# The last expert's rows added by TensorE with a 0/1 matrix, and two pieces of work moved

## The reference

```python
for i in range(8):                       # layer 0, experts; topk_idx: two experts per row
    mask = (topk_idx == i).any(-1)
    sel = jnp.sort(jnp.where(mask, tok, T))[:capacity]       # 271 rows at most
    yi = gelu(xf[sel] @ w1[i] + b1[i]) @ w2[i] + b2[i]
    out = out.at[sel].set(yi, mode='drop')                   # a later expert replaces an earlier one
x = x + out
h = layernorm(x) @ W                     # layer 1, graph step
a = leaky_relu(h @ attn_l + (h @ attn_r).T, 0.2)
nomi = exp(a - a.max(1)) * adj
x = x + elu((nomi / nomi.sum(1)) @ h)
```

## Time and profile before

| | us |
|---|---|
| median of three runs | 875.61 |
| lowest and highest run | 867.36, 879.09 |
| profiled execution, its own time | 869.55 |
| its span in the trace | 867.7 |

### The profile page before, as it was taken

The page is one execution under the profiler, slowest core; times in us unless marked ns, Lnnn a source line. Parts: engine busy times, 40 slices in busy tenths (PEclk is TensorE's granted clock), DMA queues, the critical chain, the costliest instruction groups (busy, mean ns, idle before and its releaser), DMA issues. The chain is left out here.

```text
span 867.7 us, 13717 instructions
## 1 busy us (share of the span) xinstructions
PE 775.2 (89%) x4212; PEld 585.6 (67%) x4213; DVE 603.2 (70%) x1175; ACT 409.1 (47%) x836; POOL 337.3 (39%) x333
## 2 busy tenths in 40 slices
PE   5999999999999999935999984899958999999994
PEld 4998655555545543424999982687846888888883
DVE  6675867766675679984989865687694656666562
ACT  3345435556555556631666641641332544444451
POOL 2600258668667778434424005000011444333422
PEclk9998979999999999975999995999868999999997
DMA  7538877888887866333345303951472388752110
GB/s 272 202 100 314 208 238 255 272 270 254 279 276 251 282 235 220 128 96 108 137 154 214 124 26 111 433 205 56 169 300 90 67 263 237 240 156 38 31 19 0
DMA packets 61655, 159.02 MB, mean 183 GB/s; under 512 B 20907, under 2 KB 39521, under 8 KB 58403
## 3 DMA queue, kind: packets, MB, share of 16 engines
q1 hardware_dynamic: 40659, 97.97, 33.3%
q0 software_dynamic: 20944, 60.38, 22.6%
HBM read 103.00 MB, written 49.93 MB: 176 GB/s over the span
## 5 line engine op out<-in xcount | busy, mean ns | idle before, releaser
L1868 DVE TENSOR_REDUCE mx<-ps 128x1 f32<-128x452 f32 x264 | 147.8, 622 | 66.3 <-PE ps L1317 65.6
L973 ACT ACTIVATE expo<-ps 128x452 f32<-128x452 f32 x264 | 124.4, 552 | 96.1 <-PE ps L1329 95.2
L1337 PE MATMUL ps<-expo,v_st 128*64 128x452 f32 (+1 forms) x576 | 117.1, 528 | 0.0
L1161 ACT ACTIVATE h<-ps,b_l 128x128 f32<-128x128 f32 x224 | 60.8, 383 | 115.4 <-PE ps L1677 112.5
L1317 PE MATMUL ps<-k_st,q_st 96*128 96x452 f32 x264 | 108.9, 425 | 4.1 <-DVE mx L1868 3.8
L1329 PE MATMUL ps<-q_st,k_st 98*128 98x452 f32 x264 | 96.7, 390 | 3.4 <-ACT expo L973 2.3
L907 POOL DMA_INDIRECT out<-y1t,out_row x29 | 46.1, 1591 | 118.3 <-DVE share L2264 94.7
L1317 PEld LDWEIGHTS ps<-k_st,q_st 96*128 96x128 f32 x264 | 51.1, 194 | 52.6 <-DVE mx L1868 34.7
L1694 PE MATMUL ps<-w_ring,h_hi 128*128 x232 | 82.6, 395 | 1.3 <-DVE h_lo L2276 0.5
L837 POOL TENSOR_TENSOR part_lo<-part,part_hi 128x512 fp32r<-128x512 f32 x64 | 82.3, 1312 | 0.5
L890 POOL DMA_INDIRECT x1t<-x_d,goal x29 | 30.0, 1033 | 128.8 <-DVE goal L2238 110.8
(11 more groups left out here) (352 smaller groups left out, 1793.2 us busy)
## 6 DMA issues: line engine op xcount, KB each, us to landing
w_l<-w_l SPq DMA_DIRECT2D x8, 2053.0 KB, 8.4
part<-w_l POOLq DMA_DIRECT2D x32, 512.0 KB, 6.5
w_split_d<-part_hi POOLq DMA_DIRECT2D x32, 512.0 KB, 5.4
w_split_d<-part_lo POOLq DMA_DIRECT2D x32, 512.0 KB, 3.9
adj<-adj_t SPq DMA_DIRECT2D x22, 704.0 KB, 4.3
w_ring<-w_split_d SPq DMA_DIRECT2D x10, 1365.5 KB, 6.7
w_ring<-w_split_d SPq DMA_DIRECT2D x5, 1365.0 KB, 6.2
w_ring<-w_split_d SPq DMA_DIRECT2D x1, 4096.0 KB, 13.6
```

Source lines behind the costliest of these rows:

```text
L973: act.activation(expo[g % 8][:, :], ps[:, 3 + g % 3, 0:QC], ACT.Exp, scale=SCALE).then_inc(s_exp, 1)
L1161: last = act.activation(h1[:, f, :], ps[:, 4 + f // 4, (f % 4) * P:(f % 4 + 1) * P], ACT.Gelu_apprx_tanh, bias=b1_l1[:, bass.ds(e, 1), f])
L1337: return pe.matmul(ps[at:at + 2 * DK, 6 + g // T % 2, lo:hi], v_st[h % 2][:, kt, :], expo[g % 8][:, lo:hi], start=kt < 2, stop=kt == T - 1 ...
L1868: dve.tensor_reduce(mx4[:, n // KB, n % KB:n % KB + 1], ps[:, i % 3, 0:KC], AX_X, ALU.max).then_inc(s_mx, 1)
```

## The change

Seven experts' results are gathered from memory; the eighth's is not written to memory at all. The gathers wait for the first seven results only, and their bounds check leaves out rows of expert 7, whose tiles keep zeros. ScalarE writes the token numbers plus 128 of all tiles into `numbers` (eleven activations, during the seventh expert). VectorE compares them with `place_of0` of expert 7's three row blocks, which gives `hot_last`, a matrix with a 1 where a slot holds a token. The eighth result is kept in SBUF as a high part `y_hi` (ScalarE) and a low part `y_lo` (VectorE); TensorE multiplies `hot_last` with both, two tiles to a PSUM bank, and VectorE adds each pair of tiles to `x_res` (`last_expert`). VectorE's order after the experts is: comparison, five gathered tiles, low part, two gathered tiles, and then the groups with the other gathered tiles between them. The addition of `u` and the products with the attention vectors stand ahead of the experts. TensorE takes the right and left scores of each group right behind its turning, and the first two features behind the third turning. SyncE's load of the edge weights also waits for the comparison and the high part.

```diff
-RIGHT_BANKS = (7, 7, 3)
+RIGHT_BANKS = (7, 3, 7)
+LAST_AT = (E - 1) * CT
+EARLY_ROWS = 5
...
-        RIGHT_DONE, LEFT_DONE = (1, 3, 4), (2, 5, 6)
+        RIGHT_DONE, LEFT_DONE = (1, 3, 5), (2, 4, 6)
...
+                    if last and k:
+                        continue
                     sp.wait_ge(s_yo, PRIMED + e + 1)
...
             sp.wait_ge(s_y0_ps, PRIMED + E)
+            sp.wait_ge(s_w2lo, E + 1)
+            sp.wait_ge(s_yo, PRIMED + E)
             for t in range(T):
                 sp.wait_ge(s_gath[t], 16)
...
-                pool.wait_ge(s_ys[k], PRIMED + 32 * (E // 2))
+                pool.wait_ge(s_ys[k], PRIMED + 32 * len(range(k, E - 1, 2)))
             for t in range(T):
                 pool.indirect_dma_start(
-                    out=nat[:, t, :], out_offset=None, in_=ys0_d[:, :],
+                    out=nat[:, t, :], out_offset=None, in_=ys0_d[0:SLOTS0 - CAPP, :],
...
+            def token_numbers():
+                act.wait_ge(s_w2lo, E - 1)
+                for t in range(T):
+                    act.activation(numbers[:, t, :], const[:, C_IOTA:C_IOTA + P], ACT.Identity, bias=const[:, C_FAR + t:C_FAR + t + 1])
+
+            def last_rows():
+                act.wait_ge(s_yo_ps, PRIMED + E)
+                act.activation(y_hi[:, 0:2, :], ps[:, 6, :].rearrange("p (s d) -> p s d", d=D), ACT.Identity)
+                act.activation(y_hi[0:CREM, 2, :], ps[0:CREM, 7, 0:D], ACT.Identity).then_inc(s_yo, 1)
...
                     weights_high(1 - k, i * 16 + (16 if k == 0 else 32))
+                if numbered:
+                    token_numbers()
                 act.wait_ge(s_y0_ps, PRIMED + e + 1)
...
-            rows_out(E - 1, 1, (E // 2 - 1) * 32)
+            last_rows()
...
+            for c in range(DT):
+                for kt in range(DT):
+                    mm = pe.matmul(ps[:, 2, 2 * c:2 * c + 2], w_graph_t[:, kt, c * P:(c + 1) * P], attn_lr[:, kt, :],
+                                   start=kt == 0, stop=kt == DT - 1)
+            mm.then_inc(s_small, 1)
             xs_in(0, 0, 16 * CT)
...
+            pe.wait_ge(s_w2lo, E + 1)
+            pe.wait_ge(s_yo, PRIMED + E)
+            for p in range(-(-T // 2)):
+                tiles = range(2 * p, min(2 * p + 2, T))
+                for y in (y_hi, y_lo):
+                    if y is y_lo:
+                        pe.wait_ge(s_xt, E + 1)
+                    for t in tiles:
+                        n = min(P, N - t * P)
+                        for c in range(CT):
+                            w = P if c < CT - 1 else CREM
+                            mm = pe.matmul(ps[0:n, p, (t % 2) * D:(t % 2 + 1) * D], hot_last[0:w, c, t * P:t * P + n],
+                                           y[0:w, c, :], start=y is y_hi and t % 2 == 0 and c == 0,
+                                           stop=y is y_lo and t == tiles[-1] and c == CT - 1, skip_group_check=True)
+                mm.then_inc(s_xt_ps, 1)
...
             turn_group(1)
+            right(1)
+            left(1)
+            turn_group(2)
             features(0, 2)
-            turn_group(2)
-            right(1)
             right(2)
-            left(1)
             left(2)
...
             row_number(sa)
+            dve.tensor_tensor(x_res[:, :, :], x_res[:, :, :], u[:, :, :], ALU.add).then_inc(s_x2, 1)
+            dve.wait_ge(s_small, WAL_DONE)
...
-            dve.tensor_tensor(x_res[:, :, :], x_res[:, :, :], u[:, :, :], ALU.add).then_inc(s_x2, 1)
-
-            dve.wait_ge(s_small, WAL_DONE)
...
+            dve.wait_ge(s_yt, PRIMED + E - 1)
+            for c in range(CT):
+                w = P if c < CT - 1 else CREM
+                last = dve.tensor_scalar(hot_last[0:w, c, :], numbers[0:w, :, :].rearrange("p t n -> p (t n)")[:, 0:N],
+                                         place_of0[0:w, LAST_AT + c:LAST_AT + c + 1], None, ALU.is_equal)
+            last.then_inc(s_w2lo, 1)
...
+            gathered(0, EARLY_ROWS)
+            dve.wait_ge(s_yo, PRIMED + E)
+            dve.tensor_tensor(y_lo[:, 0:2, :], ps[:, 6, :].rearrange("p (s d) -> p s d", d=D), y_hi.bitcast(F32)[:, 0:2, :],
+                              ALU.subtract)
+            dve.tensor_tensor(y_lo[0:CREM, 2, :], ps[0:CREM, 7, 0:D], y_hi.bitcast(F32)[0:CREM, 2, :],
+                              ALU.subtract).then_inc(s_xt, 1)
+            gathered(EARLY_ROWS, EARLY_ROWS + 2)
+
+            def last_expert(p):
...
+                dve.wait_ge(s_xt_ps, E + p + 1)
+                dve.wait_ge(s_x2, summed[0])
+                dve.tensor_tensor(x_res[0:n, 2 * p:2 * p + k, :], x_res[0:n, 2 * p:2 * p + k, :],
+                                  ps[0:n, p, 0:k * D].rearrange("p (k d) -> p k d", d=D), ALU.add).then_inc(s_x2, 1)
...
             normed_group(0)
+            gathered(EARLY_ROWS + 2, 8)
             normed_group(1)
-            group_max(0)
+            gathered(8, T)
             normed_group(2)
-            group_max(1)
-            group_max(2)
+            for n in range(3):
+                group_max(n)
```

More of the change, by code:

```diff
@@ L271, in build_program @@
         y0 = [place(f"y0_{i}", [CT, D]) for i in range(2)]
+        cursor[0] = offsets["w_l0_0"]
+        numbers = place("numbers", [T, P])
+        assert cursor[0] <= offsets["w_l0_0"] + B1AT * 4
+        cursor[0] = offsets["w_hi0"]
+        hot_last = place("hot_last", [CT, N], F32R)
+        assert cursor[0] <= offsets["w_hi1"]
+        cursor[0] = offsets["xs0_0"]
+        y_hi, y_lo = place("y_hi", [CT, D], F32R), place("y_lo", [CT, D], F32R)
+        assert cursor[0] <= offsets["w_hi0"]
         cursor[0] = offsets["nt"]
@@ L1039, in rows_out, with expert0 @@
                 act.activation(y0[k][0:CREM, 2, :], ps[0:CREM, 7, 0:D], ACT.Identity).then_inc(s_yo, 1)
-            def expert0(i, k, first=False, more=True):
+            def token_numbers():
[6 more added lines that the diff above has]
+                act.activation(y_hi[0:CREM, 2, :], ps[0:CREM, 7, 0:D], ACT.Identity).then_inc(s_yo, 1)
+            def expert0(i, k, first=False, more=True, numbered=False):
                 e = i * 2 + k
@@ L1100, in _ @@
             normed_group(2)
+            turned_group(2)
             features(0, FIRST_FACTORS)
-            turned_group(2)
             for n in range(3):
@@ L2009, in _ @@
             row_number(sa)
+            dve.tensor_tensor(x_res[:, :, :], x_res[:, :, :], u[:, :, :], ALU.add).then_inc(s_x2, 1)
+            dve.wait_ge(s_small, WAL_DONE)
+            dve.tensor_copy(left_wide[:, :, :], ps[:, 2, 0:2 * DT].rearrange("p (c n) -> p c n", n=2)[:, :, 0:1]
+                            .to_broadcast([P, DT, P])).then_inc(s_wal_sb, 1)
+            dve.tensor_copy(right_wide[:, :, :], ps[:, 2, 0:2 * DT].rearrange("p (c n) -> p c n", n=2)[:, :, 1:2]
+                            .to_broadcast([P, DT, P])).then_inc(s_wal_sb, 1)
+            dve.tensor_copy(w_graph[:, :, D:D + 2], ps[:, 2, 0:2 * DT].rearrange("p (c n) -> p c n", n=2)).then_inc(s_wal_sb, 1)
             def xs_t(e):
@@ L2057, in _, with gathered @@
             expert0(E // 2 - 1, 1, more=False)
[L2058 to L2069 removed]
+            dve.wait_ge(s_yt, PRIMED + E - 1)
[4 more added lines that the diff above has]
+            last.then_inc(s_w2lo, 1)
+            summed = [1]
+            def gathered(lo, hi):
                 for t in range(lo, hi):
@@ L2072, in normed_group @@
                     dve.tensor_tensor(x_res[:, t, :], x_res[:, t, :], nat[:, t, :], ALU.add).then_inc(s_x2, 1)
-                    if t > lo:
-                        dve.wait_ge(s_x2, 1 + t)
-                        dve.bn_stats(stats[:, t - 1, :], x_res[:, t - 1, :])
-                dve.wait_ge(s_x2, 1 + hi)
-                step(dve.bn_stats(stats[:, hi - 1, :], x_res[:, hi - 1, :]))
+                    summed[0] += 1
+            gathered(0, EARLY_ROWS)
[6 more added lines that the diff above has]
+            def last_expert(p):
+                n = min(P, N - 2 * p * P)
+                k = min(2, T - 2 * p)
+                dve.wait_ge(s_xt_ps, E + p + 1)
+                dve.wait_ge(s_x2, summed[0])
+                dve.tensor_tensor(x_res[0:n, 2 * p:2 * p + k, :], x_res[0:n, 2 * p:2 * p + k, :],
+                                  ps[0:n, p, 0:k * D].rearrange("p (k d) -> p k d", d=D), ALU.add).then_inc(s_x2, 1)
+                summed[0] += 1
+            def normed_group(n):
+                lo, hi = ROW_GROUPS[n]
+                for t in range(lo, hi, 2):
+                    last_expert(t // 2)
+                    dve.wait_ge(s_x2, summed[0])
+                    for r in range(t, min(t + 2, hi)):
+                        last = dve.bn_stats(stats[:, r, :], x_res[:, r, :])
+                step(last)
                 for t in range(lo, hi):
```

18 lines of the change are left out of this document (5 added, 13 removed).

## The result

| | us |
|---|---|
| before, median of four runs (867.36 to 879.09) | 872.16 |
| after, median of four runs (886.20 to 896.98) | 889.90 |
| ratio of the runs, 95% interval | 1.0224, 1.0175 to 1.0273 |
| profiled execution of after, its own time and span | 896.98, 895.2 |

The change made the kernel slower: by 889.90 - 872.16 = 17.7 us, or, by the ends of the interval, 15.3 to 23.8 us. Whether the loss is over 2% the interval leaves open; the prediction gave that a chance of 0.02. Forecast were 874.7 us and a range of 866 to 882. The change does what it says, and most steps of the prediction came out as worked out, but one was wrong by a factor of three, and the clock cost more than the upper end that it was given.

A forecast was written before the change was run, and what follows sets the result against it. The bound was TensorE's 13.65 us idle before group 0's turning, while the last result went through memory. Earlier maximum -3.1, addition ahead of the experts +2.0, token numbers +0.2: -0.9 us from 875.61 gives 874.7, range 866 to 882.

The forecast's parts named there:

- The other sixty: Products of the 0/1 matrix after the first six: at most 0.125 us each, 7.5 us at the full clock.
- The clock: TensorE's granted clock during the last expert's products: a loss of 2.0 us, between nothing and 4.45.
- Rival 3: Clock stays low for the 8.9 us it took before: 1.6 us slower, 877.2 us, chance 0.10.
- The rest of TensorE's order: TensorE from turning group 0 to the last group maximum: 14.9 us, the maximum 3.1 us earlier than before.
- The reordered spread products: Score and feature products in new order on TensorE: as long as before, at no cost.
- the gathers during the eighth expert: GpSimd's first gather of the last stage starts 2.77 us behind the seventh result's second store, at 511.06.
- the low part: VectorE's low part of the last result, behind five gathered additions: ready at 521.3, including 0.8 us for held-back gathers.
- the second gather of the first expert: Start of the experts: gather held back by VectorE's moved addition, delaying TensorE 2.0 us, bounds 0 and 3.1.
- the token numbers: Eleven ScalarE activations ahead of the seventh transposed result: 2.95 us and fit, or 5.5 and delay 2.5; taken at 0.2.
- VectorE's share as hidden cover: VectorE's additions and normed tiles hidden behind TensorE's products: no cost, or 0 to 2 us if the cover is gone.
- Rival 2: Gathers held back wherever they meet VectorE, 3.1 us at the start, 4.5 beside the comparisons: 879.5 us, chance 0.18.
- Rivals 1 and 4: Nothing collides and the clock stays up: 869.7 us, chance 0.22; gathers don't start during the eighth expert: 884.8, 0.03.

## Why the prediction was wrong

**The step that failed** is "The other sixty cost at most the 0.125 us between the starts of two expert matmuls": 7.5 us, measured 24.3. I took the rate from products that all have 128 rows on both sides of each start, and called it an upper bound because these have more columns. The sixty have forty changes between 128 and 16 rows (four in six products). The trace of before has such changes too, in a line that I read without its weight loads: turning an expert's rows in (`xs_in`) takes blocks of 128, 128 and 16 rows, twice. In a middle expert of before, at a granted clock of 1.00, beside the turning of a result (`rows_out`), whose six all have 128 rows (TensorE's timeline and that of its weight loads):

```profile
411.64 1.07 PE L1469 MATMUL ps<-const,xs 128*128 128x128 f32 x6
421.90 0.82 PE L1487 MATMUL ps<-const,y_t 128*128 128x128 f32 x6
...
411.95 0.36 PEld L1469 LDWEIGHTS ps<-const,xs 16*128 16x128 f32 x3 [0.17 <-issue]
```

The load of 16 rows begins 0.17 us late here as well. An estimate from these lines, (1.07 - 0.82) / 3 = 0.08 us for a change and 3.3 us for forty, is less than half of what a change cost in the sixty at that clock (0.19), but it would have told of a cost that the 0.125 us leaves out.

The 24.3 us split with the numbers of the experiments: sixty at the full clock without a change 60 / 6 x 0.71 = 7.1, near the 7.5 of the forecast; half the clock all the way adds 10 x (1.28 - 0.71) = 5.7; forty changes at half the clock add 40 x 0.30 = 11.9; together 24.7.

The Trainium skill (TensorE: Matmul & The Clock Gate, "Step-by-step: what each phase is for") lets a weight load run beside the product ahead of it where row groups don't conflict or the load goes into a second buffer, and says that the row count doesn't matter for its duration. The durations nearly agree (in the sixty of after 0.28 us for a load of 16 rows, 0.31 in the mean for one of 128). A change of the number of rows is not among the conditions of that section, but here the load does not run ahead at one: the trace shows 0.22 us of idle time, and the measurement decides.

**The clock** was taken at 2.0 us with an upper end of 4.45, from the 8.9 us that it took to come back before. The end was no bound: it stayed at 0.50 for some 30 us of work in after. By the split above it cost 5.7 us on the products alone, and 40 x (0.30 - 0.19) = 4.4 more on the changes. Why it stayed low is not shown: with such changes it did in five traces of five, without them it fell in three of six and came back while the products ran. Rival 3, the clock low for longer, named the right direction, with too low a price and for too short a stretch.

**The rest of TensorE's order** was given 14.9 us from the turning to the last maximum. In the kernel with 128 rows it takes 14.58; in after 17.14, since the clock is still low for the turning (1.97 us instead of 1.04) and the first right product (3.64 instead of 1.8). The same kernel settles the products as well: 14.64 us to the turning against 530.8 - 516.09 = 14.71 forecast. With the third block padded, the whole sum up to the last maximum is that of the prediction. In part that is luck: in this trace the clock fell for about as long as I had assumed. In the two traces with the same products in which it did not fall, group 0 is turned at +12.29 and +12.41.

**A cost that I set at nothing**: "The reordered spread products take as long as before; they cost nothing because they stand in this sum." They do take as long, but what follows them was not read. With the features 2 and 3 behind the last left product, TensorE stops 3.03 us for ScalarE's copies, the clock falls (0.66 in the window 580 to 584), and the eleven graph weights take 1.3 us longer in after (39.00 instead of 37.66): they take 38.7 to 40.0 us in all eight traces with this order and these banks, against 37.6 to 37.7 in the three with the old order.

**Right**: the gathers during the eighth expert (2.84 us behind the seventh's second store at 520.91, forecast 2.77); the low part 5.0 us behind the transposed result (begun at 532.71, ended at 533.71), forecast 521.3 - 516.09 = 5.2; the second gather of the first expert (+1.98, forecast 2.0, and confirmed by the run that moved the addition); the token numbers, which took 3.31 us and fit: ScalarE's copy begins at 515.88, about 0.1 us behind the seventh expert's last product (515.44 + 0.29 = 515.73), forecast 0.2 (the +0.11 of the whole stage shows nothing by itself, since that stage varies from 116.4 to 117.6 us over the traces); VectorE's share as hidden cover: where the products run pair by pair, TensorE never waits ahead of the turning of group 0, even at the full clock, and where the high part goes first it waits 2.22 us, against a price of 0 to 2. Rival 2, the gathers held back wherever they meet VectorE, was wrong: beside the comparisons they lost 0.58 us (0.22 + 0.36), not 4.5, and at the start the first gather was not caught (1.09 us, as before). A lock that is held for one instruction, as the prediction tells it, does not give these upper ends: no gather waited for more than the rest of one operation. Rivals 1 and 4 fall with the same rows.

## What to carry to other kernels

When a row is to price a new product, compare the number of rows with that of its neighbours in the order, not only its columns: a short last block between full ones costs a pause at both of its ends, and padding it with zeros cost nothing that a stage shows here. A rate from the same engine is an upper bound only if the new sequence has the same shapes side by side. And where an order is changed, follow it past the event at which the sum ends: the next engine's copies may now come too late.

## What was not expected of the hardware

- Two products in a row with 128 and 16, or 128 and 64 rows: 0.18 to 0.19 us for each change at the granted clock of 1.00, 0.30 us at 0.50, as a mean of both directions; at 0.50 the weight load behind a change begins 0.22 us late, whichever way the change goes, with "issue" as the reason.
- The granted clock stayed at 0.50 through 19 to 24 us of products with changes in between, in all five kernels that have them, though PE counted as busy throughout; in the kernels without them it came back during the products or never fell.
- Three comparisons of 1354 columns took 2.57 us, 0.86 each, against 1.49 worked out from the addition's rate, and the two gathers beside them took 0.22 and 0.36 us longer; an addition of two SBUF tensors held one back by 1.9 us.
- Stages with the same code differ by up to 3 us from trace to trace (273.3 to 276.3 from the eleventh graph weights to the end), so a microsecond there is no evidence for a change.
